# Graph attention on one core: the short VectorE operations, the weighted product and the exponential change their places within a step

## What is computed

```python
h = (x @ W).reshape(n, HEADS, C)
s_src = jnp.einsum('nhc,hc->nh', h, a_s)
s_dst = jnp.einsum('nhc,hc->nh', h, a_d)
e = jax.nn.leaky_relu(s_src[src] + s_dst[dst], NEG_SLOPE)
m = jax.ops.segment_max(e, dst, num_segments=n)
ex = jnp.exp(e - m[dst])
denom = jax.ops.segment_sum(ex, dst, num_segments=n)
alpha = ex / denom[dst]
msg = h[src] * alpha[:, :, None]
out = jax.ops.segment_sum(msg, dst, num_segments=n)
```

## Time and profile before

| what | value |
|---|---|
| median of two runs | 8447.11 us (8445.72 to 8448.5) |
| the profiled execution | 8452.29 us, its span 8450.6 us |
| graph attention's three layers of steps | about 6056 to 6775, 6850 to 7570 and 7640 to 8391 us of the span |
| busy over the span | PE 68%, PEld 55%, DVE 63%, ACT 35%, POOL 62% |
| granted TensorE clock, mean | 0.888 of full speed |

### The profile page before, as it was taken

The page is one execution under the profiler, slowest core; times in us unless marked ns, Lnnn a source line. Parts: engine busy times, 40 slices in busy tenths (PEclk is TensorE's granted clock), DMA queues, the critical chain, the costliest instruction groups (busy, mean ns, idle before and its releaser), DMA issues. The chain is left out here.

```text
span 8450.6 us, 153428 instructions
## 1 busy us (share of the span) xinstructions
PE 5775.2 (68%) x32873; PEld 4645.0 (55%) x33057; DVE 5350.2 (63%) x15356; ACT 2998.2 (35%) x7461; POOL 5261.2 (62%) x5324
## 2 busy tenths in 40 slices
PE   0005445546547945997997997898588878887886
PEld 0004435534336844776776776777366656655664
DVE  8003346664441227777776777777688868887888
ACT  0001100000012214444444444444466646655664
POOL 4777777757712125776776776776367646656764
PEclk9996677767778977999999999999799989999998
DMA  6001123323308942343443443443233323323332
GB/s 228 10 2 47 53 70 102 103 80 104 103 24 295 370 153 81 105 106 101 105 105 100 105 105 100 105 106 96 69 93 94 89 78 93 93 74 94 94 92 72
DMA packets 597889, 866.01 MB, mean 102 GB/s; under 512 B 273775, under 2 KB 412013, under 8 KB 596374
## 3 DMA queue, kind: packets, MB, share of 16 engines
q0 software_dynamic: 233280, 595.84, 25.6%
q1 hardware_dynamic: 364502, 269.16, 10.6%
HBM read 740.80 MB, written 125.75 MB: 103 GB/s over the span
## 5 line engine op out<-in xcount | busy, mean ns | idle before, releaser
L1766 POOL DMA_INDIRECT hs<-tab_agnn,rec x1952 | 1900.1, 973 | 653.6 <-issue 559.2
L2209 POOL DMA_INDIRECT hs<-tab_gat,rec x1464 | 1521.7, 1039 | 680.1 <-issue 417.2
L1832 DVE CUSTOM_DVE_ANT_0 prod<-psG,hs 128x256 f32<-128x256 f32 x1952 | 829.1, 481 | 404.9 <-DMA hs<-tab_agnn,rec 324.2
L1895 PE MATMUL psG<-HN,ohT 128*128 x3904 | 966.1, 391 | 12.8 <-DVE lg L1832 5.8
L2241 DVE TENSOR_REDUCE mt<-psL 128x2 f32<-128x1024 f32 x732 | 860.0, 1215 | 142.9 <-PE psL L2362 84.8
L1912 PE MATMUL psV<-hs,pr 128*128 128x258 f32 x3904 | 934.0, 383 | 0.0
L1895 PEld LDWEIGHTS psG<-HN,ohT 128*128 128x128 f32 x3904 | 710.6, 192 | 107.7 <-issue 20.3
L1849 ACT ACTIVATE prT<-cand,mn 128x512 f32<-128x512 f32 x488 | 352.4, 722 | 1170.2 <-DVE mn L1792 1157.9
L1912 PEld LDWEIGHTS psV<-hs,pr 128*128 128x128 f32 x3904 | 707.8, 191 | 80.9
L2378 PE MATMUL psV<-msg,oh 128*128 128x260 f32 x2928 | 730.4, 394 | 1.0 <-DVE msg L2286 0.6
L805 PE MATMUL psT<-ident,oh 128*128 128x128 f32 x416 | 101.6, 391 | 847.8 <-DVE oh L770 847.8
(11 more groups left out here) (346 smaller groups left out, 12120.4 us busy)
## 6 DMA issues: line engine op xcount, KB each, us to landing
w<-in_L_gnn_w SPq DMA_DIRECT2D x224, 512.0 KB, 6.0
hs<-tab_agnn,rec POOLq DMA_INDIRECT x1952
fwd_d<-acc SPq DMA_DIRECT2D x10, 2730.0 KB, 34.1
fw<-fwd_d SPq DMA_DIRECT2D x104, 260.0 KB, 2.8
hs<-tab_gat,rec POOLq DMA_INDIRECT x1464
rec<-rec_d SPq DMA_DIRECT2D x1166, 10.0 KB, 1.8
b<-in_L_gnn_b SPq DMA_DIRECT2D x113, 128.0 KB, 6.4
x<-xbuf SPq DMA_DIRECT2D x112, 128.0 KB, 6.0
```

The costliest lines, as they stand in the source:

```text
L1766: nc.gpsimd.indirect_dma_start(out=hs[:, j, g, :], out_offset=None, in_=k.tab_agnn, in_offset=bass.IndirectOffsetOnAxis(ap=rec[:, j, g, 0: ...
L1832: ins = V.tensor_tensor_reduce(prod[:, h2, g, :], psG[:, bank(j2, half), m, :], hs[:, j2, g, 0:D], hs[:, j2, g, D:D + 1], 0.0, ALU.mult, A ...
L1895: mm = nc.tensor.matmul(psG[:, bank(j1, half), m, :], ohT[:, j1 % 2, 2 * half + m, :], pick(HN, b, slice(None)).rearrange("p a c -> p (a c ...
L2209: nc.gpsimd.indirect_dma_start(out=hs[:, j, g, :], out_offset=None, in_=k.tab_gat, in_offset=bass.IndirectOffsetOnAxis(ap=rec[:, j, g, 0:1 ...
```

## The change

It touches the three streams DVE, ACT and PE of graph attention's steps; no operation is computed otherwise, except that `leaky` is split in two (16 columns for group s-4, 4 columns for group s-3). On DVE, `raw` from `psQ` (2258) comes directly after the reductions, the operations of groups s-4, s-6 and s-3 alternate, and the split-off `leaky` and `df` of group s-3 come at the end of the step, behind `msg`. On ACT the exponential (2317) becomes the first instruction of the step, ahead of `away`, and `oh` (2313) the last, behind `neg`. On PE `psV` (2378) becomes the first part of the step, ahead of the transposes, and both pairs of `psL` stand together.

```diff
 DVE
                             top(0)
                             top(1)
+                            if old:
+                                dve.wait_ge(q.q, own(t) + 1)
+                                V.tensor_tensor(g3(raw, now), hrow[:, :, :, C_HEAD], q3[:, :, 0, :], ALU.add).then_inc(s_lg, 1)
                             if add:
...
                                 V.tensor_tensor(a4, a4, b3(rs[:, j6, :], CH1), ALU.mult).then_inc(s_am, 1)
+                            if old:
+                                dve.wait_ge(s_lg, own(t) + 1)
+                                V.scalar_tensor_tensor(out=leaky[:, now, 0:GH], in0=raw[:, now, 0:GH], scalar=NEG_SLOPE,
+                                                       in1=raw[:, now, 0:GH], op0=ALU.mult, op1=ALU.max).then_inc(s_leak, 1)
                             if mid_:
                                 dve.wait_ge(s_lt, pairs(t2) + 2)
                                 V.tensor_tensor(at_block(smax, b), at_block(smax, b), mt[:, h2, :], ALU.max).then_inc(s_mx, 1)
+                            if old:
+                                dve.wait_ge(s_leak, pairs(t) + 2)
+                                V.tensor_tensor(g3(t3, h), g3(leaky, now), q3[:, :, 1, :], ALU.subtract).then_inc(s_t3, 1)
+                            if mid_:
                                 dve.wait_ge(s_mx, own(t2) * 2 + 1)
                                 V.tensor_tensor(raw[:, now, GH:], at_block(smax, b), at_block(sd, b), ALU.add).then_inc(s_mx, 1)
...
                             if old:
                                 dve.wait_ge(s_t3, own(t) + 1)
                                 V.tensor_scalar(t3[:, h, :], t3[:, h, :], 60.0, None, ALU.min).then_inc(q.tt, 1)
                             if add:
+                                dve.wait_ge(s_am, own(t6) + 1)
                                 dve.wait_ge(q.v, nth(t6) + 1)
-                                dve.wait_ge(s_am, own(t6) + 1)
                                 V.tensor_tensor(acc, acc, psV[:, j6 % 2, 0:W_GAT], ALU.add).then_inc(q.u, 1)
                             if old:
                                 dve.wait_ge(q.e, flow(t) + 1)
...
                                                 ALU.mult).then_inc(q.msg3, 1)
+                            if mid_:
+                                if not (isinstance(t2, int) and t2 < 1):
+                                    dve.wait_ge(q.m, flow(t2))
+                                dve.wait_ge(s_mx, own(t2) * 2 + 2)
+                                V.scalar_tensor_tensor(out=leaky[:, now, GH:], in0=raw[:, now, GH:], scalar=NEG_SLOPE,
+                                                       in1=raw[:, now, GH:], op0=ALU.mult, op1=ALU.max).then_inc(s_leak, 1)
+                                if not (isinstance(t2, int) and t2 < 2):
+                                    dve.wait_ge(q.rs, flow(t2 - 1))
+                                dve.wait_ge(s_leak, pairs(t2) + 1)
+                                V.tensor_tensor(df[:, h2, :], at_block(peak, b), leaky[:, now, GH:], ALU.subtract).then_inc(q.df, 1)
 ACT
                         def step(i, j):
+                            if old:
...
+                                act.wait_ge(q.tt, own(t) + 1)
...
+                                nc.scalar.activation(weights, t3[:, h, :], ACT.Exp).then_inc(q.e, 1)
                             if now:
...
                                 nc.scalar.activation(neg[:, h1, :], psT[:, 0, :], ACT.Copy, scale=-BIG).then_inc(q.ev, 1)
+                            if old:
+                                act.wait_ge(s_away, own(t) + 1)
+                                nc.scalar.activation(flat(oh, h), flat(away, j4), ACT.Relu, bias=1.0, scale=-1.0).then_inc(q.oh, 1)
 PE
                         def step(i, j):
+                            if add:
+                                _, j5, t5 = add
+                                h5 = j5 % 2
+                                pe.wait_ge(q.msg3, own(t5) + 1)
+                                pe.wait_ge(q.oh, nth(t5) + 1)
...
+                                mm.then_inc(q.v, 1)
                             if last:
...
                                 pair(0)
-                            if add:
...
-                            if mid_:
                                 pair(1)
```

More of the change, by code:

```diff
@@ L2175, in graph_attention @@
                     spread = lambda t: layer * (NG * 2) + (L2_LAYERS * NG + t * 2)
-                    step_of = lambda t: layer * (NG + 1) + t
                     def at_block(v, b):
@@ L2296, in step @@
                             now, last, mid_, old = (lagged(i, j, n) for n in (0, 1, 3, 4))
+                            if old:
+                                _, j4, t = old
+                                h = j4 % 2
+                                if not (isinstance(t, int) and t < 2):
+                                    act.wait_ge(q.v, nth(t - 1))
+                                act.wait_ge(q.tt, own(t) + 1)
+                                weights = msg[:, h, :, :].rearrange("p g (h c) -> p (g h) c", h=HEADS)[:, :, C_HEAD]
+                                nc.scalar.activation(weights, t3[:, h, :], ACT.Exp).then_inc(q.e, 1)
                             if now:
@@ L2306, in step @@
                                 ins.then_inc(s_away, 1)
[L2307 to L2317, removed]
                             if mid_:
@@ L2346, in step @@
                             last, mid_, low, add = (lagged(i, j, n) for n in (1, 2, 3, 5))
+                            if add:
[3 more added lines that the diff above has]
+                                pe.wait_ge(q.oh, nth(t5) + 1)
+                                if not (isinstance(t5, int) and t5 < 2):
+                                    pe.wait_ge(q.u, added(t5 - 1))
+                                for g in range(G):
+                                    mm = nc.tensor.matmul(psV[:, h5, 0:W_GAT], oh[:, h5, g, :], msg[:, h5, g, :],
+                                                          start=(g == 0), stop=(g == G - 1))
+                                mm.then_inc(q.v, 1)
                             if last:
```

## The result

The changed kernel takes 8646.5 us (median of two runs, 8643.93 to 8649.07) against 8447.11 us: 2.35% slower, ratio 1.0235 with a 95% interval of 1.0217 to 1.0253, or +199 us. The forecast was +133 us. The profiled execution has a span of 8642.2 us. From the first to the last `msg` a layer takes 783.9, 784.3 and 783.1 us where it took 717.1, 717.1 and 717.3; three times 66.6 is 200 us, the whole difference of the medians. (The two profiled spans differ by 191.6 us only, because in this execution the first layer began 8.3 us earlier.)

What follows compares the result with a forecast made beforehand. DVE's own order of instructions was taken to set the time. Ordinary steps -6, turn +48, chain +34 and clock +60 gave +136 us, 8583 against the median, stated as 8580; range 8455 to 8700.

Steps and rivals of the forecast that it cites:

- border of 2%: Whole kernel: slower than 8616 us had chance 0.31, faster than 8278 us 0.02, between them 0.67.
- DVE's ordinary step: DVE's steps without the loop's turn: 5.60 us instead of 5.62, the gain eaten behind `msg`; -6 us over 306 steps.
- The turn: DVE at the loop's turn: branch and reload lie open behind `df`; net +0.8 us for 60 turns, +48 us.
- The chain: From `df` through ACT's `oh` and PE's `psV` to a reduction: 6.29 us, 0.29 us late; +34 us.
- The clock: TensorE falls to the 1.2 GHz level in one stretch per turn, about 1.0 us each; 60 us.
- A: Rival on TensorE: the clock stays up; +76, or +20 with a shorter chain, 8467 to 8523 us; chance 0.23.
- C: Rival on DVE: faster, `leaky` to `df` to reduction takes 0.30 us, not 0.70; about 8425 us; chance 0.08.
- D: Rival on DVE: spacing dependent operations gains nothing, 0.72 us not saved; +262, 8709 us; chance 0.03.
- B: Rival on PE: low clock twice in a turn and in ordinary steps too; +244, 8690 us; chance 0.20.

Runs made afterwards that it cites:

- e7: Against the changed kernel: DVE's 4-column `leaky` ahead of the accumulator addition, `df` ahead of `msg`; ACT and PE as before the change. 8273.1 us, ratio 0.9781.
- e1: The changed kernel with PE's old order, `psV` between the two pairs of `psL` again; DVE and ACT as changed. 8434.8 us, ratio 0.9979.
- e5: The changed kernel with twelve unused identity matmuls on PE ahead of `psV`'s waits for `msg` and `oh`. 8564.8 us, ratio 1.0127.
- e4: The changed kernel with DVE's 4-column `leaky` ahead of the accumulator addition and `df` ahead of `msg`. 8350.2 us, ratio 0.9873.
- e3: DVE's part of the change alone, ACT and PE as in the kernel before. 8462.8 us, ratio 1.0010.
- e2: The changed kernel with ACT's `oh` behind `away` instead of last in the step; DVE and PE as changed. 8511.0 us, ratio 1.0053.

## Why the prediction was right, and where its sizes were off

The direction and the mechanism held: slower, through the chain from `df` over ACT's `oh` and PE's `psV` to the reduction, with the open turn and the lower clock as the other two terms. The time lies inside the range; the forecast was 66 us too low, and a border of 2% that it gave two chances in three not to be crossed was crossed. (The prediction took 2% for about what can be told from no change; the interval is 0.2% either way.) Part of the hit is luck: the gain in DVE's own step was taken 68 us too small, which hid more than half of the 47 and 59 us by which the chain and the clock were taken too small. Term by term, from the table of steps:

- **DVE's ordinary step.** Forecast 5.60 us; in time it is 5.50 in the changed kernel. `raw` to `msg` is 1.44 for the forecast 1.51, `leaky` to `df` 0.30 as forecast, `df` to the reduction 0.27 for 0.40. The 0.21 us of register work at line 224 lie open (0.207 us from 7107.72, the reduction at 7107.97), but the hand-overs around it are smaller than taken. 273 x -0.27 is -74 us where the sum had -6. Of the 0.25 us between the two, 0.10 is the new step (5.50 for 5.60); 0.15 is the old one, which the sum took from the single step of the earlier trace rows, 5.62, where the mean ordinary step before is 5.77. The gain stays small because of the two operations behind `msg`; e7 shows what it is without that.
- **The turn.** Forecast +0.8 each, measured +0.88. Of this +0.67 is DVE's own, as in e1: the 17 turns with the clock up ahead of the reduction take 7.57 us, the 40 at the lower level 7.87. The reload begins behind `df`, as worked out; in the changed kernel it shares its time with the wait for `psL`.
- **The chain.** Forecast 6.29 us from `df` to the reduction a step on; 6.40 in the pair of steps at full clock above. What was off was the step it is held against: with 5.43 us and 0.27, not 5.60 and 0.40, the reduction could have started 5.70 after that `df`, so it is 0.70 late and not 0.29. Late and in-time steps alternate, as said. 108 late steps by 0.75 (6.25 less 5.50) are +81 us for the forecast 34.
- **The clock.** I took one stretch per turn at 1.0 us, 60 us. What failed is the count: 127 stretches at the lower level instead of 35, about two per turn, half of them beginning in a turn or in the step behind it and half in the steps between. 68 ordinary steps are very late, by 1.74 us each over the late ones (7.99 less 6.25), +119 us, and 40 turns lose 0.30, +12, which is 1.2 us for each of the 108 stretches that begin in these steps. In an ordinary step it is more than I took, since my 1.0 us counted `psV` alone, while transposes and pair behind it run at the same clock: 5.03 us from `psV` to the reduction in the pair of steps above where 3.36 (7151.37 to 7154.73) is the time at full clock:

```profile
7151.37 2.02 PE L2354 MATMUL psV<-msg,oh 128*128 128x260 f32 x8 [1.22 <-ACT oh L2337]
```

Together -74 + 81 + 119 = +126 us for the ordinary steps, and 50 for the turns, 12 of them the clock's. The two losses that were taken too small outweigh the gain that was taken too small.

Of the rivals, A (the clock stays up) is out by the trace, C (`df` to the reduction under 0.15) by its 0.27, D (spacing gains nothing) by e7 and by 5.47 us in e1. B gave the cause of the excess rightly, two stretches in a turn and ordinary steps at the lower level, with 1.4 us each where it was 1.2; its 8690 was 44 us too high, nearer than the forecast's 66 too low. The trace now shows a clock that goes down and up again on average once in three steps, with idles of 1.22 us in front of `psV`. What the Trainium skill (TensorE: Matmul & The Clock Gate, A second HAM failure mode) says of short idles that recur is of the same kind; its case is one that cycles through PSUM, while here PE idles for ScalarE.

Not settled: how much of these 131 us an always full clock would give back, and why a wait of the same length sometimes leaves the clock up. e5 gives back 82 with work of its own in the chain; a kernel with a full clock and no added work was not tried.

## What to carry to other kernels

In this software pipeline the place of an instruction at the end of a step mattered more than its length (e4): whatever feeds the next engine belongs ahead of the long operation, and an engine's last instruction should not be one whose result another engine needs at its head. Register work and the reload at a loop's turn want a long operation as the last thing issued before them (1.1 us of idle per turn in e7, 2.2 in e1). Before engines' orders are changed together, run each alone and in pairs: here the good part (spaced short operations, 2.2% faster by e7) was eaten by `leaky` and `df` behind `msg` in DVE's own new order (e3: 0.1% slower), and ACT's and PE's parts lengthened the chain on top of it.

## What the runs showed that I had not expected

The lower clock comes and goes with the places of the loop. A wait of about 1.2 us in front of `psV` is often followed by a lower clock, but not always: 114 such waits (1.15 to 1.3 us) met a full clock, and in 72 of them it fell in the wait or within 2 us of the start of `psV`. Of the two chains shown above, behind the same 1.22 us, one takes 8.06 us and the other 6.40. In e2, e4 and e5 every very late step stands at one place, the second step behind a turn. Twelve useless matmuls a step took 82 us off. And e7, the fastest version, has a clock of 1.00 in the first layer, where the kernel before had 0.98, and no late ordinary step.
